# Code search on one core: the low halves move from VectorE to TensorE and ScalarE, and the eight PSUM banks are dealt out anew

## The reference, cut to what matters

```python
# x: (8, 64, 256, 256) f32
x = x + _L0_conv_ref(_gn(x), weights1, weights2)   # group norm, 2-D DCT, 64x32 modes mixed over channels, inverse DCT
x = x + _L1_conv_ref(_gn(x), embeddings)           # group norm, nearest of 1024 codes for each 64 values

def _L1_conv_ref(x, embeddings):                   # embeddings (D=64, K=1024)
    flat = x.reshape(-1, D)
    distances = sum(flat * flat, 1) + sum(embeddings ** 2, 0) - 2.0 * flat @ embeddings
    codes = argmin(distances, axis=1)
    return embeddings.T[codes].reshape(x.shape)
```

## Time and profile before

| | us |
|---|---|
| median of 3 runs | 7373.56 |
| lowest, highest | 7361.45, 7394.95 |
| profiled execution, its own time | 7382.31 |
| its span in the trace | 7380.5 |
| busy: PE, DVE, ACT, POOL | 6392.3, 6776.5, 4352.2, 5114.3 |
| mean granted PE clock | 0.887 of 2.4 GHz |

### The profile page before, as it was taken

The page is one execution under the profiler, slowest core; times in us unless marked ns, Lnnn a source line. Parts: engine busy times, 40 slices in busy tenths (PEclk is TensorE's granted clock), DMA queues, the critical chain, the costliest instruction groups (busy, mean ns, idle before and its releaser), DMA issues. The chain is left out here.

```text
span 7380.5 us, 130164 instructions
## 1 busy us (share of the span) xinstructions
PE 6392.3 (87%) x24080; PEld 2436.6 (33%) x24080; DVE 6776.5 (92%) x18796; ACT 4352.2 (59%) x11681; POOL 5114.3 (69%) x4614
## 2 busy tenths in 40 slices
PE   7998788888888888888888888888898888888887
PEld 3458233333223333333333333333333333333232
DVE  7771699999999999999999999999999999999998
ACT  2331566656666666666666666666666666666665
POOL 0000577777877777777777777777777777777777
PEclk9998889888998888888988888988888888889987
DMA  7979455555555555555555555555555555555554
GB/s 253 307 252 186 97 143 137 132 130 135 134 142 132 137 135 134 135 141 136 134 134 138 138 136 134 134 140 135 137 132 134 135 137 137 137 135 136 139 135 106
DMA packets 1110238, 1073.54 MB, mean 145 GB/s; under 512 B 690656, under 2 KB 830752, under 8 KB 1109472
## 3 DMA queue, kind: packets, MB, share of 16 engines
q1 hardware_dynamic: 895968, 651.56, 33.0%
q0 software_dynamic: 196608, 411.30, 25.0%
q10 hardware_dynamic: 16896, 4.20, 0.3%
HBM read 722.32 MB, written 143.01 MB: 117 GB/s over the span
## 5 line engine op out<-in xcount | busy, mean ns | idle before, releaser
L980 POOL DMA_INDIRECT arena<-table,idx x4096 | 4237.7, 1035 | 1451.9 <-issue 1215.2
L673 ACT ACTIVATE arena<-bank 128x512 f32<-128x512 f32 x4096 | 2432.3, 596 | 2421.3 <-PE bank L515 2340.1
L515 PE MATMUL bank<-eh,t 128*128 128x512 f16 x8192 | 2764.6, 422 | 830.9 <-DVE mx L872 605.2
L872 DVE CUSTOM_DVE_ANT_0 arena<-bank,arena 128x512 f32<-128x512 f32 x4096 | 2771.4, 677 | 160.3 <-ACT arena L673 108.3
L882 DVE FIND_INDEX8 idx<-mx,arena 128x8 uint32<-128x512 f32 x4096 | 2811.0, 686 | 0.0
L515 PE MATMUL bank<-el,t 67*128 67x512 f16 x8192 | 2747.7, 420 | 0.0
L515 PEld LDWEIGHTS bank<-eh,t 128*128 128x128 f16 x8192 | 629.7, 105 | 2851.4 <-ACT arena L673 1766.8
L515 PEld LDWEIGHTS bank<-el,t 67*128 67x128 f16 x8192 | 873.7, 107 | 1186.6 <-issue 377.1
L987 POOL TENSOR_TENSOR X<-X,arena 128x1024 f32<-128x1024 f32 x256 | 606.2, 2368 | 13.7 <-DVE arena L909 7.8
L494 PE MATMUL conv<-X,ident 128*128 128x512 f32 x1024 | 598.1, 668 | 5.8 <-ACT Ts L610 5.8
L499 PE MATMUL conv<-iw,Ts 64*128 64x512 f32 x1024 | 599.2, 666 | 0.0
(11 more groups left out here) (102 smaller groups left out, 3915.6 us busy)
## 6 DMA issues: line engine op xcount, KB each, us to landing
X<-x SPq DMA_DIRECT2D x512, 512.0 KB, 4.5
y<-X SPq DMA_DIRECT2D x256, 512.0 KB, 3.0
t<-t SPq DMA_DIRECT2D x256, 256.0 KB
arena<-table,idx POOLq DMA_INDIRECT x4096
arena<-w SPq DMA_DIRECT2D x12, 2048.0 KB, 22.8
arena<-w SPq DMA_DIRECT2D x64, 128.0 KB, 3.0
spec<-Fs SPq DMA_DIRECT2D x256, 16.0 KB, 3.5
Xc<-spec SPq DMA_DIRECT2D x16, 256.0 KB, 8.6
```

What stands on the lines that cost most here:

```text
L515: last = nc.tensor.matmul(bank[4 + k % 2 if e else k % 4][:], tile[0:rows, g.buf2, k], codes[0:rows, e], start=rows == P, stop=rows != P)
L673: nc.scalar.activation(R[:, k % 4], bank[4 + k % 2][:], ACT.Relu).then_inc(b_rl, 1)
L872: V.tensor_tensor_reduce(out=Fm[:, k % 4], in0=bank[k % 4][:], in1=R[:, k % 4], scale=1.0, scalar=-3.0e38, op0=ALU.add, op1=ALU.max, accum ...
L980: G.indirect_dma_start(out=q[:, g.buf2, k], out_offset=None, in_=table, in_offset=bass.IndirectOffsetOnAxis(ap=idx[:, g.buf2, k, 0:1], axis=0)
```

## The change

VectorE's subtraction `low_half` goes. TensorE makes the low halves instead: the identity times `Y` (fp32), plus a new f16 constant `nid16` (minus the identity) times the high halves, accumulated in the two banks of `conv`, one matmul pair behind k = 5 and one behind k = 6; ScalarE copies the 1024 columns to `YS` as f16 behind k = 7 (`take_low`). For this `conv` has to be free then, so the inverse transform moves to k = 10 to 13. `inverse_h` and `statistics` get a bank of their own, `aux`, which was the fourth bank of the even scores: these now rotate over three banks. `score_lag` is how many tiles back the `best` is that must be done: 3, but 2, 2 and 5 for the first three tiles of each round of eight groups, where 128 tiles over three banks don't come out even. The chain of the second norm is taken apart: `take_x` is behind k = 14, `square_sum`, `statistics`, `delta2_of`, `variance_of` and `inverse_deviation` come a group later than before (for g+2, in k = 1, 4, 5, 5 and 7), `scale_of` and `bias_of` behind 13, and `high_half` behind 15 of the group before the one in which it stood. Groups 0 to 3 are primed accordingly.

```diff
+        aux = bank[3]
...
+        nid16 = sb("nid16", [P, P], F16)
...
+        def score_bank(g, k):
+            return bank[(NT * (g.r % U) + k) % 3]
+        def score_lag(g, k):
+            return {0: 2, 1: 2, 2: 5}.get(NT * (g.r % U) + k, 3)
...
-            def inverse_h(g):
+            def inverse_h(g, known):
                 need(pe, m_in[g.buf2], 16 * (g.visit(2) + 1))
-                need(pe, b_x1, g.n)
+                need(pe, b_ve, known)
+                need(pe, b_t, g.n)
                 hold(pe, "pe", g.n)
-                nc.tensor.matmul(conv[0:CG * MY, 1, 0:T2 * P], M[:, g.buf2], ih[:], start=True,
+                nc.tensor.matmul(aux[0:CG * MY, 0:T2 * P], M[:, g.buf2], ih[:], start=True,
                                  stop=True).then_inc(b_inv, 1)
...
-                    need(pe, b_ve, g.n)
+                    need(pe, b_x1, g.n)
+                    need(pe, b_yl, g.n - 1)
...
-                nc.tensor.matmul(conv[:, 0, 0:2], avg_all[:], sums[:], start=True, stop=True).then_inc(b_st, 1)
+                need(pe, b_ve, g.n)
+                hold(pe, "pe", g.n)
+                nc.tensor.matmul(aux[:, 0:2], avg_all[:], sums[:], start=True, stop=True).then_inc(b_st, 1)
+            def low_half(g, t, taken):
+                if t == 0:
+                    need(pe, b_y, g.n + 1)
+                    need(pe, b_x1, taken)
+                    hold(pe, "pe", g.n)
+                ks = slice(t * (NT // T2), (t + 1) * (NT // T2))
+                cv = conv[:, t].rearrange("p (k d) -> p k d", d=D)
+                nc.tensor.matmul(cv, ident[:], Y[:, g.buf4, ks], start=True, stop=False)
+                nc.tensor.matmul(cv, nid16[:], YS[:, ks, 0:D], start=False, stop=True).then_inc(b_low, 1)
             def scores(g, k):
                 n = NT * g.n + k
                 if k == 0:
                     need(pe, t2_in[g.buf2], 16 * (g.visit(2) + 1))
                     hold(pe, "pe", g.n)
-                need(pe, b_ttr, n - 3)
+                need(pe, b_ttr, n - score_lag(g, k) + 1)
                 need(pe, b_rl, n - 1)
                 for rows, tile, codes in ((P, t1, eh), (D + 3, t2, el)):
                     for e in range(2):
-                        last = nc.tensor.matmul(bank[4 + k % 2 if e else k % 4][:], tile[0:rows, g.buf2, k],
+                        last = nc.tensor.matmul(bank[4 + k % 2][:] if e else score_bank(g, k)[:],
+                                                tile[0:rows, g.buf2, k],
                                                 codes[0:rows, e], start=rows == P, stop=rows != P)
                 last.then_inc(b_sc, 1)
...
-                    g, three, four = Group(i, r), Group(i, r + 3), Group(i, r + 4)
+                    g, one, two, three, four = (Group(i, r + n) for n in range(5))
                     for k in range(NT):
                         scores(g, k)
+                        if two.exists() and k == 4:
+                            statistics(two)
+                        if one.exists():
+                            if k == 5:
+                                low_half(one, 0, two.n + 1 if two.exists() else NG)
+                            if k == 6:
+                                low_half(one, 1, NG)
                         if three.exists():
-                            if k == 4:
+                            if k == 10:
                                 add_x(three, 0)
-                            if k == 5:
+                            if k == 11:
                                 inverse_w(three, 0)
-                            if k == 6:
+                            if k == 12:
                                 add_x(three, 1)
-                            if k == 7:
+                            if k == 13:
                                 inverse_w(three, 1)
-                            if k == 14:
-                                statistics(three)
-                        if four.exists() and k == 15:
-                            inverse_h(four)
+                        if four.exists() and k == 14:
+                            inverse_h(four, four.n - 1)
...
+            def take_low(g):
+                need(act, b_low, T2 * (g.n + 1))
+                nc.scalar.copy(YS[:, :, D:2 * D], conv[:].rearrange("p t (k d) -> p (t k) d", d=D)).then_inc(b_yl, 1)
...
-                        if before.exists() and k in (10, 12, 13, 14):
+                        if before.exists() and 9 <= k < 9 + TA // 2:
                             for n in range(2):
-                                sum_product(before, NT - TA + 2 * (10, 12, 13, 14).index(k) + n)
+                                sum_product(before, NT - TA + 2 * (k - 9) + n)
                         if one.exists():
-                            if k == 0:
-                                high_half(one)
                             if k == 2:
                                 normalise(one)
+                            if k == 7:
+                                take_low(one)
                         if two.exists():
-                            if k == 8:
+                            if k == 1:
+                                square_sum(two)
+                            if k == 5:
+                                delta2_of(two)
+                            if k == 13:
                                 scale_of(two)
-                            if k == 8:
                                 bias_of(two)
+                            if k == 15:
+                                high_half(two)
                         if three.exists():
-                            if k == 1:
+                            if k == 0:
                                 take_t(three)
-                            if k == 9:
+                            if k == 14:
                                 take_x(three)
-                            if k == 11:
-                                square_sum(three)
-                            if k == 15:
-                                delta2_of(three)
...
-            def low_half(g):
-                need(dve, b_y, g.n + 1)
-                hold(dve, "dve", g.n)
-                V.tensor_tensor(YS[:, :, D:2 * D], Y[:, g.buf4], YS[:, :, 0:D], ALU.subtract).then_inc(b_yl, 1)
...
-                before, one, three = (Group(g.i, g.r + n) for n in (-1, 1, 3))
+                before, two = Group(g.i, g.r - 1), Group(g.i, g.r + 2)
                 slot = 2 * k + at
                 if before.exists():
                     if slot == 12:
                         choose(before)
                     if slot == 30:
                         settle(before)
-                if one.exists() and slot == 7:
-                    low_half(one)
-                if three.exists():
-                    if slot == 31:
-                        variance_of(three)
+                if two.exists():
+                    if slot == 11:
+                        variance_of(two)
...
-                        if three.exists() and k == 15:
-                            inverse_deviation(three)
+                        if two.exists() and k == 7:
+                            inverse_deviation(two)
```

More of the change, by code:

```diff
@@ L520, in body_b, with inverse @@
                 for r in range(U):
-                    g, three, four = Group(i, r), Group(i, r + 3), Group(i, r + 4)
+                    g, one, two, three, four = (Group(i, r + n) for n in range(5))
                     for k in range(NT):
                         scores(g, k)
+                        if two.exists() and k == 4:
[5 more added lines that the diff above has]
+                                low_half(one, 1, NG)
                         if three.exists():
-                            if k == 4:
+                            if k == 10:
                                 add_x(three, 0)
-                            if k == 5:
+                            if k == 11:
                                 inverse_w(three, 0)
-                            if k == 6:
+                            if k == 12:
                                 add_x(three, 1)
-                            if k == 7:
+                            if k == 13:
                                 inverse_w(three, 1)
-                            if k == 14:
-                                statistics(three)
-                        if four.exists() and k == 15:
-                            inverse_h(four)
-            for r in range(3):
-                inverse_h(Group(0, r))
-                for t in range(T2):
[L541 to L544, removed]
+                        if four.exists() and k == 14:
+                            inverse_h(four, four.n - 1)
+            def inverse(g):
+                for t in range(T2):
+                    add_x(g, t)
+                    inverse_w(g, t)
+            inverse_h(Group(0, 0), 0)
+            inverse(Group(0, 0))
+            statistics(Group(0, 0))
+            inverse_h(Group(0, 1), 1)
+            for t in range(T2):
+                low_half(Group(0, 0), t, 1)
```

(32 more changed lines are left out.)

8 lines of the change are left out of this document (5 added, 3 removed).

## The result

The changed kernel takes 7917.68 us (median of 4 runs, 7913.11 to 7936.62) against 7367.51 (4 runs, 7343.56 to 7394.95) of the kernel before: 1.075 times as long, interval 1.071 to 1.079. The forecast was 7565, 2.6% slower, with a range up to 7830. The direction is as forecast, and so is the mechanism, except for the place and the cost of the low clock; the time lies 88 us past the range.

What follows compares the result with a forecast made beforehand. Taken as bounds: DVE (92% busy), with the gather ending the first half, then PE's chain after the change. 25.6 + 0.8 clock + 0.2 loop turns - 0.2 = 26.4 us a group against 25.64, 192 us more: 7565, range 7290 to 7830.

Steps and rivals of the forecast that it cites:

- (1): DVE: `low_half` leaves, 1.12 us a group, 287 us in all if nothing else waits.
- (2): DVE's products wait for the gather until T + 9.7 (T: step 0 on DVE); 0.3 of 1.12 us is left.
- (3): PE's two low halves behind k = 5 and 6: 1.12 us each, costing nothing behind the gather wait.
- (4): Three even score banks in place of four: PE's lead is worth 1.3 us, where it was 2.6.
- (5): Inverse matmuls at k = 10 to 13: PE's chain makes a group 25.6 us; DVE alone would give 24.9.
- (6): ACT's copy of the low halves, 1.01 us, starts the transposing DMA near T + 10.2, not 6.56; nothing waits.
- (7): POOL's moved `inverse_deviation`, shorter search lags (at most 45 us) and start-up (under 10 us): all taken as 0.
- (8): PE's clock: an even share of low clock on steps 10 to 15 costs 1.0 us, taken 0.8, bounds 0 and 3.
- D: Rival: long low-clock stretches on PE's steps 10 to 15 in every group, 3 us more, some 8130 us; chance 0.07.
- C: Rival: PE, 2.2 us fuller, keeps its clock; 25.8 us a group, 41 us more, 7415 us; chance 0.08.
- A: Rival: the gather wait before the products eats the gain, but PE keeps up; 7297 to 7373 us; chance 0.20.
- B: Rival: full gain on DVE, gathers land by T + 8.4 and PE keeps up; 7087 us; chance 0.04.

Runs made afterwards that it cites:

- e1: Kernel before without any low half (low part of `YS` stays zero, the transposing DMA waits for `Y`): 7297.64 us, 0.989.
- e6: Changed kernel without the four low-half matmuls on PE; ACT still copies the two banks: 8016.09 us, 1.088.
- e5: Kernel before with three even score banks and the change's lags, nothing else: 7363.94 us, 1.0003.
- e4: Changed kernel with the inverse transform earlier: `add_x` and `inverse_w` of half 0 behind step 9, the second pair behind 10 and 11: 7491.43 us, 1.016.
- e12: Changed kernel with DVE's products two steps later (k = 8), plus four useless matmuls behind step 2 and two behind 3: 7101.02 us, 0.965.
- e3: Changed kernel with eight useless f16 matmuls of 512 columns behind step 9, nothing moved: 7589.94 us, 1.029.
- e7: e4 plus five useless matmuls behind step 2 and two behind 3: 7210.65 us, 0.979.
- e10: Changed kernel with products two steps later, inverse transform at k = 9 to 12, four useless matmuls behind step 2, two behind 3: 7297.27 us, 0.991.

## Why the prediction was wrong in its size, by its own steps

(1), (2) held. The products wait in 171 of 216 groups, 0.95 us a group; in the median of the 240 groups they come at T + 9.56 (taken: 9.7), and e1 leaves 0.29 us of the 1.12 (taken: 0.3). The reason given for the earlier gather isn't shown: the profile's page of before has the gathers in a queue of their own (q0, software_dynamic), so what a transposing DMA could share with them is the 16 DMA engines, and no run moves it alone.

(3) held: 1.07 us each (taken: 1.12), hidden. e6 shows more: without them the kernel is slower.

(4) The lead of three banks was worked out as 1.3 us in place of 2.6; e5 shows that this alone costs nothing. By the order of the waits it decides how early PE may start step 10; that part wasn't measured by itself.

(5) held at full clock. Step 10 starts at 3399.02 = T + 11.78 (taken: 12.3), and steps 10 to 15 follow at 1.86, 2.03, 1.73, 2.01 and 1.55 (taken: 1.73, 2.02, 1.73, 2.02, 1.54). PE, then DVE:

```profile
3399.02 0.60 PE L542 MATMUL bank<-eh,t 128*128 128x512 f16 x2 [1.78 <-DVE mx L926]
...
3400.88 0.60 PE L542 MATMUL bank<-eh,t 128*128 128x512 f16 x2
...
3402.91 0.60 PE L542 MATMUL bank<-eh,t 128*128 128x512 f16 x2
...
3408.20 0.60 PE L542 MATMUL bank<-eh,t 128*128 128x512 f16 x2
```

```profile
3408.54 0.69 DVE L926 CUSTOM_DVE_ANT_0 arena<-bank,arena 128x512 f32<-128x512 f32 x1 [0.65 <-ACT arena L720]
...
3412.63 0.66 DVE L926 CUSTOM_DVE_ANT_0 arena<-bank,arena 128x512 f32<-128x512 f32 x1
```

The seven full-clock groups take 25.56 us where 25.6 was worked out, 0.4 more than the full-clock groups of before. DVE waits in them before `best` 14 and 15 alone (0.65 and 0.14 us in the mean), as was said. That this chain, and not the wait for the gather alone, is what the change costs at full clock is shown by e4, which shortens it to 24.59.

(6) held: `take_low` ends at T + 9.8, the transposing DMA starts at T + 10.0 (taken: 10.0 and 10.2), and PE goes from step 15 into the next group's first scores without a gap. (7) was tested in part: the shorter lags are in e5 too, which takes no longer than before.

(8) is the step that failed: "If an even share falls there". The sum gave the clock 0.8 less 0.2, and 0.2 to loop turns: 0.8 above the chain. Measured are 27.78 - 25.56 = 2.22. In e12, where low clock is nearly gone, the 229 full-clock groups have a mean 0.28 above their median (24.48 against 24.20), since the first and the last group of each eight take about 1 us more; that is what loop turns take. So the clock costs about 1.9 us where 0.6 was in the sum, and 1.3 x 256 = 333 us is nearly all of the 353 missed. The total of low clock was no error (5.8 us a group taken over from before, 5.0 measured). Its place was: a low stretch isn't spread over the group but comes right behind an idle time of PE, and the change puts the largest idle time just ahead of the densest work. The prediction named that gap, 2.3 us (1.92 in the sample group), in the same paragraph, and then averaged. A smaller part of the step failed too, that low clock before the products stays hidden: 29 groups after have low clock in their first 10.5 us alone, 6.8 us of it in the median, and take 26.93 us against the 25.56 at full clock.

Of the rivals, D had the place right, low clock on steps 10 to 15 in every group (204 of 240 have over 0.5 us of it from 10.5 us after T on), with a price of 3 us from one stretch of 13.6 us; the stretches here are mostly under 4 us (165 of 228), and the measured 7918 lies between D (8130) and mine, nearer to D. It was given 0.07. C is refuted: its clock was to stay full, and the window behind the gap shows 0.57. The Trainium skill (TensorE: Matmul & The Clock Gate, "Why this matters for your kernels") tells to leave no idle gaps of TensorE above a length that it names, so that the throughput doesn't drop. 180 of the 181 low stretches that begin from 11 to 14 us after T stand at a shorter gap than that, 2.1 us in the median, and in the sample group the clock dropped behind one of 1.92. The measurement decides: keeping to that rule isn't enough here. A and B fall with the wait of DVE for ACT, E with PE's first scores.

Of the signs named, these came: products that wait, PE's gap before step 10 and none until 15, no wait of the first scores. `best` waits from 11 on, not only at 14 and 15, since the low stretch eats the lead at once; in the seven full-clock groups it waits before 14 and 15 alone. DVE's share is 83%, not 87 to 89, since the same busy time stands in a longer span.

## What to carry to other kernels

Ask of a change what it does to TensorE's idle times, not only to its busy time: in this kernel a low stretch follows a gap, and what counts is which work stands behind the gap and whether that work has slack. A mean clock says nothing on this; this change raised it from 0.887 to 0.909 and lost 7.5%. Where a wait of one engine (here for the gather) makes another stand still, move the waiting instruction: late products are worth 93 us before and 731 after, and with them the change is 83 us better than the kernel before with the same edit (7186 against 7269), and 168 with six useless matmuls in the remaining gap.

## What the runs showed of the hardware

Useless matmuls made a kernel faster each time they were put into a gap: 7918 to 7590 (e3), 7491 to 7211 (e7), 7504 to 7297 (e10), 7186 to 7101 (e12). Taking matmuls away made it slower (e6, by 98 us: 7918 to 8016). In e4 a gap of 1.43 us behind DVE was followed by 6.8 us at 0.50, in after one of 1.92 us by less than 4; but in the full-clock group shown above a gap of 1.78 us was followed by none. What decides between the two isn't settled by these runs.
